# Down projection of a mixture of experts in split fp32: two of its three products side by side in one

## The reference, cut to what matters

```python
for e in range(NUM_EXPERTS):                       # 8
    g = jnp.einsum('th,ih->ti', t, gate_proj[e])   # 256 -> 1024
    u = jnp.einsum('th,ih->ti', t, up_proj[e])
    oe = jnp.einsum('ti,hi->th', jax.nn.silu(g) * u, down_proj[e])   # 1024 -> 256
    out = out + comb[:, e:e + 1] * oe
```

## Time and profile before

| | |
|---|---|
| median of 3 runs (lowest, highest) | 651.98 us (651.53, 652.48) |
| span of the profiled execution, first to last instruction | 645.5 us |
| the profiled execution's own time | not recorded beside its span |
| mean granted clock of TensorE | 0.926 of full speed |
| PE busy | 533.9 us, 83%, 3197 products |
| DVE busy | 378.3 us, 59% |
| POOL busy | 336.8 us, 52% |
| ACT busy | 250.4 us, 39% |

### The profile page before, as it was taken

One profiled execution on the slowest core, in us unless ns is written; L12 is line 12 of the kernel. 1 busy time (PEld: TensorE's weight loads), 2 busy tenths in 40 slices (PEclk: granted clock), 3 DMA queues, 4 the chain that ended last, 5 costly groups with the idle time before them and its releaser, 6 DMA issues.

```text
span 645.5 us, 13457 instructions
## 1 busy us (share of the span) xinstructions
PE 533.9 (83%) x3197; PEld 454.1 (70%) x3198; DVE 378.3 (59%) x896; ACT 250.4 (39%) x492; POOL 336.8 (52%) x422
## 2 busy tenths in 40 slices
PE   3489988889996515999999299999999999999770
PEld 2268877777775304888888188878878888788660
DVE  1846889999996473644334656474474434836430
ACT  1155756555553242433233252352343333425120
POOL 5346567767675465653343527466355533654320
PEclk9789999999998556899999699999999999999895
DMA  7950000000010005271121154507207211030113
GB/s 213 277 225 2 33 18 26 25 25 25 16 34 26 25 17 180 61 233 29 25 33 24 27 184 122 138 21 201 54 6 224 47 25 24 8 49 9 16 19 140
DMA packets 27090, 46.58 MB, mean 72 GB/s; under 512 B 9719, under 2 KB 22545, under 8 KB 26769
## 3 DMA queue, kind: packets, MB, share of 16 engines
q1 hardware_dynamic: 15312, 35.77, 16.7%
q0 software_dynamic: 9088, 9.52, 9.0%
q10 hardware_dynamic: 2656, 0.91, 0.7%
HBM read 36.67 MB, written 11.61 MB: 75 GB/s over the span
## 4 chain that ended last, share of the span: by engine, by line
PE 49%; DVE 25%; issue 11%; POOL 4%; DVEq 3%; DMA 3%; ACT 2%; POOLq 0%; SPq 0%; ACTq 0%
PE psum L1160 13%; PE psum L1162 13%; PE psum L1161 13%; PE psum L1190 4%; DVE split_w L949 3%; DVE picked L834 3%; DVE s_sb L796 3%; DVEq L355 2%; DVE stats L703 2%; DVE tb_hi L995 2%; PE psum L1040 2%; POOL rstd L487 2%; DMA wk<-in_wkT 1%; POOL s_sb L521 1%; PE psum L1199 1%
## 5 line engine op out<-in xcount | busy, mean ns | idle before, releaser
L1160 PE MATMUL psum<-split_w,tb_hi 128*128 x288 | 120.1, 417 | 25.6 <-DVE split_w L949 16.7
L1161 PE MATMUL psum<-split_w,tb_hi 128*128 x288 | 115.3, 400 | 0.0
L1162 PE MATMUL psum<-split_w,tb_lo 128*128 x288 | 115.3, 400 | 0.0
L1160 PE MATMUL psum<-split_w,aT_hi 128*128 x288 | 84.4, 293 | 1.3 <-DVE aT_lo L985 1.2
L1160 PEld LDWEIGHTS psum<-split_w,tb_hi 128*128 128x128 f32 x288 | 55.7, 193 | 37.9 <-issue 27.8
L1161 PE MATMUL psum<-split_w,aT_hi 128*128 x288 | 81.5, 283 | 0.0
L1162 PE MATMUL psum<-split_w,aT_lo 128*128 x288 | 81.4, 283 | 0.0
L571 POOL DMA_INDIRECT acc_rows<-o_sb,add_at x36 | 60.3, 1674 | 33.8 <-POOL add_at L569 33.8
L370 POOL TENSOR_TENSOR split_w<-w_raw,split_w (+1 forms) x8 | 46.5, 5816 | 59.1 <-DVE split_w L955 59.1
L985 DVE TENSOR_TENSOR aT_lo<-psum,aT_hi 128x512 fp32r<-128x512 f32 x72 | 46.4, 686 | 49.0 <-ACT aT_hi L678 49.0
L971 DVE TENSOR_SCALAR o_sb<-psum,blk 128x256 f32<-128x256 f32 x36 | 17.4, 484 | 96.5 <-issue 84.3
(11 more groups left out here) (158 smaller groups left out, 1077.9 us busy)
## 6 DMA issues: line engine op xcount, KB each, us to landing
w_raw<-in_experts SPq DMA_DIRECT2D x24, 768.0 KB, 4.5
w_raw<-in_experts SPq DMA_DIRECT2D x2, 3072.0 KB, 13.8
x_sb<-in_x SPq DMA_DIRECT2D x8, 256.0 KB, 5.2
z_rows<-rows SPq DMA_DIRECT2D x16, 128.0 KB, 1.7
acc_rows<-x_sb SPq DMA_DIRECT2D x16, 128.0 KB, 2.6
ceil_f<-in_mask ACTq DMA_DIRECT2D x2, 308.0 KB, 11.1
blk<-lists POOLq DMA_DIRECT2D x36, 1.0 KB
rows<-z_rows,gather_at POOLq DMA_INDIRECT x36, 4.0
```

Source lines behind the costliest of these rows:

```text
L1160: nc.tensor.matmul(dst, hi, w_hi, start=first, stop=False)
L1161: nc.tensor.matmul(dst, hi, w_lo, start=False, stop=False)
L1162: return nc.tensor.matmul(dst, lo, w_hi, start=False, stop=last)
```

## The change

The down products change their form. The high and the low image of a chunk's down weights now lie side by side in `split_w`, 256 high columns and then 256 low ones, so that high activations times both is one product of 512 columns into the whole of bank 7: the left half gets high x high, the right half high x low. A second product, low activations times the high columns, adds to the left half. Both halves are kept apart over the eight chunks, and DVE adds them when it takes them out: L971 as before for the left half, then a second instruction that multiplies the right half by the router weight and adds `y`. It waits on a new semaphore, `half_y`, until the first has written. The copies and subtractions of the down weights write into eight pieces of 256 columns, 512 apart, through `down_pair`. The low image of gate and up moves to directly behind the high one.

```diff
+        def down_pair(slot, i, n):
+
+            return weights(split_w, slot, SPLIT, 2 * GU_COLS + 2 * D * i, 2 * D * n).rearrange("p (i h d) -> p i h d", i=n, h=2)
+
+        def down_raw(slot, i, n):
+            return weights(w_raw, slot, WCOLS, GU_COLS + D * i, D * n).rearrange("p (i d) -> p i d", i=n)
+
-        def down_leftovers(engine, eng, slot, expert, at, cols):
+        def down_leftovers(engine, eng, slot, expert, i, n):

             eng.wait_ge(dn_hi, expert)
-            return engine.tensor_tensor(weights(split_w, slot, SPLIT, WCOLS + at, cols), weights(w_raw, slot, WCOLS, at, cols),
-                                        weights(split_w, slot, SPLIT, at, cols).bitcast(F32), ALU.subtract)
+            pair_ = down_pair(slot, i, n)
+            return engine.tensor_tensor(pair_[:, :, 1, :], down_raw(slot, i, n), pair_[:, :, 0, :].bitcast(F32), ALU.subtract)
...
-                nc.vector.tensor_copy(weights(split_w, slot, SPLIT, GU_COLS, DN_COLS),
-                                      weights(w_raw, slot, WCOLS, GU_COLS, DN_COLS)).then_inc(dn_hi, 1)
+                nc.vector.tensor_copy(down_pair(slot, 0, IC)[:, :, 0, :], down_raw(slot, 0, IC)).then_inc(dn_hi, 1)
                 leftovers(slot, expert, (0,))
...
-                        nc.vector.tensor_scalar(y[:, d.par, :], bank[7][:, 0:D], blk[:, number(d), 1:2].bitcast(F32), None, ALU.mult).then_inc(y_done, 1)
+                        weight = blk[:, number(d), 1:2].bitcast(F32)
+                        nc.vector.tensor_scalar(y[:, d.par, :], bank[7][:, 0:D], weight, None, ALU.mult).then_inc(half_y, 1)
+                        dve.wait_ge(half_y, number(d) + 1)
+                        nc.vector.scalar_tensor_tensor(y[:, d.par, :], bank[7][:, D:2 * D], weight, y[:, d.par, :], ALU.mult, ALU.add).then_inc(y_done, 1)
...
-                        last = three_products(bank[7][:, 0:D], aT_hi[:, par, i, :], aT_lo[:, par, i, :], parity_c,
-                                              GU_COLS + i * D, D, i == 0, i == IC - 1)
+                        nc.tensor.matmul(bank[7], aT_hi[:, par, i, :],
+                                         weights(split_w, parity_c, SPLIT, 2 * GU_COLS + 2 * D * i, 2 * D), start=i == 0, stop=False, skip_group_check=True)
+                        last = nc.tensor.matmul(bank[7][:, 0:D], aT_lo[:, par, i, :],
+                                                weights(split_w, parity_c, SPLIT, 2 * GU_COLS + 2 * D * i, D), start=False, stop=i == IC - 1, skip_group_check=True)
                     last.then_inc(y_ps, 1)
```

More of the change, by code:

```diff
@@ L323, in xattn_moe @@
                              "aT_ps", "aTh_done", "aTl_done", "y_ps", "y_done", "added"))
-        split_met = sem("split_met")
+        split_met, half_y = sem("split_met"), sem("half_y")
         dve_met, pool_met = sem("dve_met"), sem("pool_met")
@@ L527, in split @@
             def split(slot, expert):
-                down_leftovers(nc.gpsimd, pool, slot, expert, GU_COLS, DN_COLS).then_inc(w_ready, 1)
+                down_leftovers(nc.gpsimd, pool, slot, expert, 0, IC).then_inc(w_ready, 1)
             pool.wait_ge(raw_ready, 1)
-            down_leftovers(nc.gpsimd, pool, 0, 1, GU_COLS + DN_COLS // 2, DN_COLS // 2).then_inc(w_ready, 1)
+            down_leftovers(nc.gpsimd, pool, 0, 1, IC // 2, IC // 2).then_inc(w_ready, 1)
             for par in range(2):
@@ L660, in _ @@
             act_e.wait_ge(raw_ready, 1)
-            nc.scalar.activation(weights(split_w, 0, SPLIT, GU_COLS, DN_COLS),
-                                 weights(w_raw, 0, WCOLS, GU_COLS, DN_COLS), ACT.Copy).then_inc(dn_hi, 1)
+            nc.scalar.activation(down_pair(0, 0, IC)[:, :, 0, :], down_raw(0, 0, IC), ACT.Copy).then_inc(dn_hi, 1)
             split(0, 1)
@@ L948, in leftovers @@
                     dve.wait_ge(gu_hi[k], expert)
-                    nc.vector.tensor_tensor(weights(split_w, slot, SPLIT, WCOLS + at, cols),
+                    nc.vector.tensor_tensor(weights(split_w, slot, SPLIT, GU_COLS + at, cols),
                                             weights(w_raw, slot, WCOLS, at, cols),
@@ L1158, in three_products @@
                 w_hi = weights(split_w, parity, SPLIT, at, cols)
-                w_lo = weights(split_w, parity, SPLIT, WCOLS + at, cols)
+                w_lo = weights(split_w, parity, SPLIT, GU_COLS + at, cols)
                 nc.tensor.matmul(dst, hi, w_hi, start=first, stop=False)
```

2 lines of the change are left out of this document (1 added, 1 removed).

## The result

The changed kernel took 656.0 us at the median of six runs (653.0 to 656.47), the kernel before 651.46 beside it (650.3 to 652.48): a ratio of 1.0065, 95% interval 1.0050 to 1.0081. So the change costs 3 to 4.5 us, 0.5 to 0.65%. The forecast was slower, with +1.8 us and 653.8: the sign and the loss at the changes of expert are right, and the size is 40 to 57% of what was measured.

What follows compares the result with a forecast made beforehand. The prediction took the PE to set the pace in plain blocks, DVE and GpSimd at changes of expert. 3.1 + 0.7 - 2.0 = +1.8 us on the span of 645.5, plus 6.48, gave 653.8 us; range 650.8 to 656.4.

Steps and rivals of the forecast that it cites:

- DVE at the changes: At changes of expert the second weighting instruction lies uncovered on DVE's path: 0.52 us each, 3.1 us lost.
- six times: The 0.52 us of the second DVE instruction counts at the last six of seven changes of expert.
- The PE: Down products: one product fewer per chunk saves 0.0115 us, 0.092 a block, 2.0 us over 22 blocks.
- I take the sum of the measured steps, since both products stand in them as they are: Down products: a wide and a narrow one together take 0.2275 + 0.1195 = 0.3470 us, in place of 0.3585.
- without a hole: In a plain block the PE's products follow one another with no gap, so the PE sets the pace there.
- The rival of a quicker narrow product: Down products: the narrow one gains behind the wide one, 0.023 us per chunk, 4.0 us; total 651.8 us; chance 0.12.
- the one of no gain: Down products: the PE gains nothing from the pairing; +3.8 us, 655.8 us; chance 0.10.
- The end: Last two blocks: the second DVE instruction delays scatter, `aT_lo` and last `y`; between 0.52 and 0.77, taken as 0.7 us.
- The clock: Rival: the four PE waits of 1.3 us at changes draw half clock; +1.8 + 4.8, 658.6 us; chance 0.04.
- a dear second instruction: Range's upper end: 0.60 us at each of six changes plus 0.8, with no PE gain, +4.4 us.
- With the same 6.48: The median of 651.98 us lies 6.48 over the profiled span of 645.5; the same was added to 647.3.

Runs made afterwards that it cites:

- e2: The kernel before plus only the second DVE instruction, which leaves y as it was; weights, layout and products unchanged: 654.49 us, ratio 1.0058.
- e4: The changed kernel with the down-weight copy and first subtraction ahead of the weighting at a change of expert: 649.2 us, ratio 0.9977 to the kernel before.
- e3: The changed kernel without its second DVE instruction, so y comes from the first half of the bank alone: 651.57 us, ratio 1.0015 to the kernel before.
- e9: The changed kernel with TensorE waiting for the last y before the code behind the last block: 653.25 us, ratio 1.0035 to the kernel before.

## Why the prediction was right in sign and short in size

**DVE at the changes: right.** 0.52 was forecast per change; the middle four cost 2.04 / 4 = 0.51 (e2: 0.49), and e4, which takes the weighting off the path, gives it back. The 0.48 of the instruction, the 0.04 between, the copy at 1.227, GpSimd's 6.30 and the PE's wait of 1.37 are as listed. The Trainium skill (VectorE: DVE Perf Modes, Mode 2×_2P) lets an fp32 copy within SBUF take two elements a cycle, each read port one half of the outermost dimension; the trace agrees that eight pieces keep the rate, 1227 ns against 1228. The block of the 12.9 us wait cost 0.28 by the table (0.06 in e2); over all profiles it takes 24.83 to 24.93 in the changed kernel and 24.15 to 24.60 in the one before, so whether the 0.5 of "six times" came there is not shown.

**The PE: nearly the right sum, from the wrong step.** The step "I take the sum of the measured steps, since both products stand in them as they are" failed. They do not: in alternation a pair takes 0.353 and not 0.347, a block's down products 2.902 in place of 2.958 (0.056 gained, not 0.092), and the twelve gate products behind them 2.789 in place of 2.753. A plain block gained 0.02 us. There are 26 blocks that run at the PE's pace, not 22. What made up for it was not foreseen: the six blocks at the loop's turn took 9.60 to 9.69 before and take 9.45 now, 1.19 together. The block of the earlier trace rows is one of these, and its last row stands just ahead of the hole, so "without a hole" was not true of every block:

```profile
410.43 0.49 PE L1160 MATMUL psum<-split_w,tb_hi 128*128 x1
410.76 0.40 PE L1161 MATMUL psum<-split_w,tb_hi 128*128 x1
```

From the last down product (410.26) on, the steps are 0.17 and 0.33, where the changed kernel has 0.12 and 0.24 (415.67, 415.79, 416.03). The rows of TensorE's sequencer tell why. It computes the address of the next round's first gate product, before, at (times, ns min/median/max, first and last start):

```profile
L1160 PEldq FUSED_REGOPS  x1: 51/51/51, 410.3 to 410.3; - x1
```

and after:

```profile
L1168 PEldq FUSED_REGOPS  x1: 51/51/51, 414.9 to 414.9; - x1
```

Before, in all six turns, that is 0.10 us ahead of the load of the product's weights and behind the start of the last down product, so the PE waits for its sequencer; in plain blocks it is 0.3 ahead. In the changed kernel, which has eight products with their weight loads and eight addresses fewer a block, it is 0.7 to 0.8 ahead at the turns as elsewhere, in e3 too; e2 has the 0.10 of before. This fits the earlier arrival behind the last block; no run changed the sequencer's work at the turn alone. In all 0.40 + 1.19 = 1.6 for the 2.0 of the sum. The rival of a quicker narrow product would have had pairs of 0.3355, and the one of no gain pairs of 0.3585: neither came. The Trainium skill (TensorE: Matmul & The Clock Gate, Back-to-back issue gap) gives some 216 ns for an isolated product of 512 columns and 131 for one in a stream with its weight loads; here it was 227 among its own kind and 236 behind a narrow one, so the trace agrees with neither, and the measurement decides.

**The end: the mis-sized term.** 0.7 was forecast, 1.83 came. The part that was forecast is there in e9, where the index copy stands 0.3 later in the block than before and the last stretch is 24.43 (24.01 to 24.20 before), and even that is less than 0.7: `aT_lo` did not move by 0.34 but stands 1.26 us behind the start of the last transposes in both kernels (622.48 - 621.22 and 629.92 - 628.66). The other 1.2 to 1.6 is the program transfer beside the scatter. The prediction took the scatter's landing as fixed, and asked for the changes only what moves on DVE and PE, not what a shorter program on TensorE's queue will trigger.

**The clock: the rival, at another place.** At the middle changes nothing fell, as forecast. At the last change, where 3.4 us at half clock had stood behind the wait of 3.77 us, it became 6.8: with the 0.5 of the instruction, 1.33 in that block and 0.3 in the two behind, of which by difference 1.1 is the clock's. The two parts are seen singly in e2 (+0.44 in that block, with 3.4 us) and e3 (+0.82, with 6.8).

**Sum.** Changes 2.04 + 0.28 + 1.33 and the 0.30 behind the last = 3.95 for 3.1; the end 1.83 for 0.7; the PE -1.6 for -2.0; the first blocks -0.35, not forecast and within what profiles of before differ by. Together +3.8 for +1.8. That 656.0 lies inside the range is in part luck: its upper end, 656.4, was reckoned from no gain on the PE and a dear second instruction, and what filled it were the transfer beside the scatter and the clock at the last change, which it did not hold.

**The offset.** "With the same 6.48" was wrong: some 1.55 to 1.76 lie around the span, and the rest was that the profiled execution was a quick one. The difference to the median of before, +1.8, is not touched by that, but the range was laid around a span that stood for no usual run.

## What to carry to other kernels

Where an engine is not the bound in plain stretches, look for the places where it is: an instruction on DVE cost nothing in 26 blocks and its full 0.5 us at the changes of weights, and the repair was the order there, not the instruction. Price a mix of wide and narrow products by the order in which they will stand, and put like products together. When a program gets shorter, ask what its sequencer reaches earlier: the branches behind the last block drew a piece of code beside the last scatter but one, and a wait of one line took it out. Before reading a pace off one block, look one row further, and at a few blocks more: the hole at the turn stood behind the last row that was read.

## What the runs showed of the hardware that was not expected

- A 512-column product steps by 0.227 us among its own kind, by 0.236 when 256-column ones alternate with it; eight pairs in groups of four save 0.054 us a block over eight in alternation (9.447 to 9.393), 0.035 of it in the twelve 512-column products that follow.
- A 16 KB piece of program beside a scatter of 144 packets puts its landing off by 1.1 to 1.6 us (end 25.5 to 26.0 against 24.4). Sixty instructions more on TensorE ahead of it did not move the piece; a wait of TensorE ahead of the branches did (4.85 to 8.08 us into the last block).
- DVE's sequencer goes on beside a running instruction: its work takes 2.88 us ahead of a weighting that the copy follows at once, and 3.14 ahead of the copy alone, so some 0.25 of the branch and address had run beside the weighting.
- TensorE's sequencer can hold the PE up where it is not ahead: with the address computed 0.10 us ahead of the weight load a block at the loop's turn takes 9.60 to 9.69 us, with 0.7 to 0.8 ahead 9.45, as the other blocks do.
- At the wait of 2.9 to 3.9 us in front of the last change the clock fell in all thirteen profiles, and stayed at the half for 6.8 us in the six in which it fell ahead of the PE's restart (by 0.7 to 1.6 us), for 3.4 us in the seven in which it fell behind it (by 0.1 to 1.1).
- Ahead of the expert stage the clock differs from execution to execution of one kernel (0.50 or 1.00 around 205 us); the first gate product of the kernel before then starts at 251.99 in place of 248.90 or 249.77.
